# Token lists of a mixture-of-experts layer in three groups of experts instead of two, on one Trainium2 core

## What is computed

```python
k = int(CAPACITY_FACTOR * N / E)                          # 4096 / 8 = 512 tokens for each expert
route_prob = jax.nn.softmax(xf @ Ws + bs, axis=-1).T
route_vals, routes = jax.lax.top_k(route_prob, k)         # the token lists
xin = xf[routes]
h = jax.nn.gelu(jnp.einsum('ekd,edf->ekf', xin, W1) + b1[:, None, :])
out = jnp.einsum('ekf,efd->ekd', h, W2) + b2[:, None, :]
out = out * route_vals[..., None]
final = jnp.zeros((N, D)).at[routes.reshape(-1)].add(out.reshape(-1, D))
```

## Time and profile before

| | |
|---|---|
| device time, median of 3 | 803.45 us (801.62 to 807.27) |
| span of the profiled execution | 760.2 us |
| PE / DVE / ACT / POOL busy | 92% / 66% / 46% / 33% |
| search and places | end near 520.6 us of the span |
| one-hots and lists | 520.65 to 536.4 us |
| first half-width products of expert 0 | from 536.49 us |

### The profile page before, as it was taken

How to read it: one execution, slowest core, us unless ns; L and a number is a source line. 1 busy time by engine, 2 the same in 40 slices (tenths; PEclk the granted TensorE clock), 3 DMA queues, 4 the chain that set the end, 5 groups by cost and what they waited for, 6 DMA issues and landing times.

```text
span 760.2 us, 25608 instructions
## 1 busy us (share of the span) xinstructions
PE 695.7 (92%) x11058; PEld 618.6 (81%) x11058; DVE 501.5 (66%) x1159; ACT 348.2 (46%) x765; POOL 247.4 (33%) x358
## 2 busy tenths in 40 slices
PE   7998998999989999999999999508999999999993
PEld 6886787989978999899899888407689998999992
DVE  6716774555446678777767677678378878877820
ACT  2663544445544546655656564530353345325410
POOL 5510044555644413223140431001734253203333
PEclk9998999999999999999999998755899999999997
DMA  7960024343443635454544453720735255312213
GB/s 201 391 276 2 31 99 153 109 135 124 157 149 112 196 96 158 135 165 140 168 109 142 138 164 108 262 49 3 233 130 154 54 156 139 120 21 28 29 21 36
DMA packets 75467, 96.81 MB, mean 127 GB/s; under 512 B 11337, under 2 KB 67057, under 8 KB 74202
## 3 DMA queue, kind: packets, MB, share of 16 engines
q1 hardware_dynamic: 62250, 69.52, 28.0%
q0 software_dynamic: 12288, 25.12, 13.2%
q10 hardware_dynamic: 816, 0.53, 0.2%
HBM read 53.78 MB, written 41.55 MB: 125 GB/s over the span
## 4 chain that ended last, share of the span: by engine, by line
PE 78%; DVE 10%; issue 4%; DMA 3%; POOL 2%; ACT 1%; POOLq 0%; DVEq 0%
PE bank L1828 41%; PE attn L1828 27%; PE bank L1786 3%; PE bank L1880 2%; DVE arena L1488 2%; PE bank L1887 1%; DMA arena<-x_p,idxs 1%; PE attn L2189 1%; DMA big<-o_m,gidx 1%; DVE st L1043 1%; PE attn L1771 1%; PE attn L1990 1%; POOL arena L524 1%; POOL big L467 1%; DVE big L1056 1%
## 5 line engine op out<-in xcount | busy, mean ns | idle before, releaser
L1828 PE MATMUL attn<-arena 32*32 32x64 f32 (+4 forms) x6048 | 140.3, 225 | 9.2 <-issue 7.3
L1828 PE MATMUL bank<-xT,arena 128*128 128x128 f32 (+2 forms) x964 | 145.8, 306 | 0.0
L1828 PEld LDWEIGHTS attn<-arena 32*32 32x32 f32 (+3 forms) x6048 | 114.2, 120 | 33.2 <-issue 15.4
L1828 PEld LDWEIGHTS bank<-xT,arena 128*128 128x128 f32 x964 | 124.3, 192 | 11.2 <-issue 5.8
L467 POOL DMA_INDIRECT big<-o_m,gidx x64 | 71.0, 1109 | 159.7 <-PE bank L1828 116.9
L460 POOL DMA_INDIRECT x_c<-big,sidx x64 | 68.6, 1071 | 119.3 <-PE bank L1828 88.9
L1828 PE MATMUL bank<-arena,xT 128*128 128x128 f32 (+2 forms) x640 | 107.1, 320 | 0.1
L1828 PEld LDWEIGHTS bank<-arena,xT 128*128 128x128 f32 x640 | 90.0, 199 | 8.6 <-issue 2.9
L543 POOL DMA_INDIRECT out_dram<-arena,idxs x32 | 50.2, 1569 | 109.6 <-ACT arena L1010 99.3
L1165 DVE COPY_PREDICATED arena<-causal,attn 128x1024 f32<-128x1024 int32 x24 | 31.6, 1316 | 71.2 <-PE attn L1828 71.2
L524 POOL DMA_INDIRECT arena<-x_p,idxs x32 | 34.3, 1070 | 98.8 <-DVE idxs L1567 70.8
(11 more groups left out here) (305 smaller groups left out, 1249.2 us busy)
## 6 DMA issues: line engine op xcount, KB each, us to landing
x_c<-zeros SPq DMA_DIRECT2D x8, 1024.0 KB, 9.2
xT<-x_c SPq DMA_DIRECT2D x16, 512.0 KB, 4.1
o_m<-arena SPq DMA_DIRECT2D x16, 512.0 KB, 4.0
xT<-in_L_ffn_W_dram SPq DMA_DIRECT2D x8, 1024.0 KB, 7.9
gs<-in_L_ffn_W_dram SPq DMA_DIRECT2D x8, 1024.0 KB, 7.6
xT<-in_L_attn_x_dram SPq DMA_DIRECT2D x8, 512.0 KB, 5.2
out_dram<-xT SPq DMA_DIRECT2D x8, 512.0 KB, 5.2
arena<-in_L_attn_x_dram SPq DMA_DIRECT2D x7, 512.0 KB, 6.2
```

The lines of the kernel that those rows point to most:

```text
L1828: return nc.tensor.matmul(out_, l, r, start=a, stop=z, skip_group_check=True)
```

## The change

There are three groups: expert 0 alone, experts 1 to 3, and experts 4 to 7. The table of a group is copied (`by_digits`) inside the next group's first `one_hots`, between the high digit's one-hot and the multiplication by the token number. The tables go to banks 4, 5 and 3, and expert 0's first products to banks 4 to 7, so that they no longer share banks 2 and 3 with the lists. PE does the second half of group 2's table and its `spread` inside `first_hidden`, and the wait for all lists moves from before the first half product to before `rows_t(1)`.

```diff
-LISTS = ((0, 4), (4, 8))
+LISTS = ((0, 1), (1, 4), (4, 8))
...
-                    nc.scalar.activation(ht[:, 0, f, :], bank[2 + f % 4][:, :], ACT.Gelu_apprx_tanh,
+                    nc.scalar.activation(ht[:, 0, f, :], bank[4 + f % 4][:, :], ACT.Gelu_apprx_tanh,
...
-            def one_hots(q, h):
+            def one_hots(q, h, after_digits=lambda: None):
...
                                         over_e(number[:, :, at], hi - lo), ALU.is_equal)
+                after_digits()
                 dve.wait_ge(s_low, 2 * q + h + 1)
...
-            for q in range(NL):
-                for h in range(2):
-                    one_hots(q, h)
-                    if q and h == 0:
-                        by_digits(q - 1)
-                        token_list(q - 1)
+            one_hots(0, 0)
+            one_hots(0, 1)
+            for q in range(1, NL):
+                one_hots(q, 0, lambda: by_digits(q - 1))
+                token_list(q - 1)
+                one_hots(q, 1)
             by_digits(NL - 1)
             token_list(NL - 1)
...
             by_lists(1, 0)
             warm(5, bank[7])
             by_lists(1, 1)
+            warm(5, bank[7])
+            spread(1)
+            by_lists(2, 0)
             warm(8, bank[7])
...
-                    ins = mm(bank[2 + f][:, t], w1s[0][:, k, P * f:P * f + P], xet[:, 0, k, t], k == 0, k == 1)
+                    ins = mm(bank[4 + f][:, t], w1s[0][:, k, P * f:P * f + P], xet[:, 0, k, t], k == 0, k == 1)
...
                 first_rows_t(0)
-                spread(1)
-                warm(6, bank[5])
-                pe.wait_ge(s_list, NL)
+                by_lists(2, 1)
                 pe.wait_ge(e_xt, 1)
                 hidden_half(0, 0)
                 hidden_half(1, 0)
+                spread(2)
                 first_rows_t(1)
                 hidden_half(2, 0)
+                pe.wait_ge(e_xt, 2)
+                for f in range(3):
+                    hidden_half(f, 1)
                 hidden_half(3, 0)
-                pe.wait_ge(e_xt, 2)
-                for f in range(4):
-                    hidden_half(f, 1)
+                hidden_half(3, 1)
+                pe.wait_ge(s_list, NL)
                 rows_t(1)
...
                 if n:
                     pe.wait_ge(h_c, 3 * n)
-                else:
-                    pe.wait_ge(e_gl, 5)
...
-                if n == 0:
-                    pe.wait_ge(e_gl, 6)
...
+LIST_BANK = (4, 5, 3)
```

More of the change, by code:

```diff
@@ L1561, in by_digits @@
                 dve.wait_ge(s_idx, q + 1)
-                nc.vector.tensor_copy(cidx[0:n * HI, q, 0:n * LO], bank[3 + q][0:n * HI, 0:n * LO]).then_inc(s_idxc, 1)
+                nc.vector.tensor_copy(cidx[0:n * HI, q, 0:n * LO], bank[LIST_BANK[q]][0:n * HI, 0:n * LO]).then_inc(s_idxc, 1)
             def token_list(q):
@@ L2157, in by_lists @@
                 for t in range(NT // 2 * h, NT // 2 * h + NT // 2):
-                    ins = mm(bank[3 + q][0:n * HI, 0:n * LO], oha[:, lo:hi, :, t].rearrange("p e c -> p (e c)"),
+                    ins = mm(bank[LIST_BANK[q]][0:n * HI, 0:n * LO], oha[:, lo:hi, :, t].rearrange("p e c -> p (e c)"),
                              ohb[:, lo:hi, :, t].rearrange("p e c -> p (e c)"), t == 0, t == NT - 1)
@@ L2226, in first_hidden @@
                     for k in range(2):
-                        ins = mm(bank[2 + f % 4][:, :], w1s[0][:, k, P * f:P * f + P], xet[:, 0, k, :], k == 0, k == 1)
+                        ins = mm(bank[4 + f % 4][:, :], w1s[0][:, k, P * f:P * f + P], xet[:, 0, k, :], k == 0, k == 1)
                     ins.then_inc(e_h, 1)
```

## The result

| | before | changed |
|---|---|---|
| median of 9 executions, us | 803.45 (800.79 to 807.27) | 798.11 (792.21 to 799.49) |
| ratio, with its 95% interval (the two medians alone give 0.9934) | | 0.9923 (0.9902 to 0.9943) |
| profiled execution: own time / span, us | not recorded / 760.2 | 799.49 / 797.7 |

The account below looks back on a forecast made before the run. PE was taken as the bound, with a 1.09 us wait for expert 1's gather before its steady stretch. Its queue, re-added, brought expert 1's transposes from 546.40 to 545.1: 803.45 − 1.3 = 802.1 us, range 799.4 to 804.8.

Parts of the forecast that it names:

- the 43.25 us between lie outside the span and are not touched: Whole run: the difference between the 760.2 us span and the 803.45 us median was held to stay unchanged.
- The narrow product: Expert 0's table on PE: 0.034 us per 32-column product, scaled from 128 columns; 1.1 us for 32.
- First list and first gather: DVE's first list at 524.65, 3.9 us earlier at its end; POOL's first gather at 525.65.
- The 96-column product: Table of experts 1 to 3 on PE: 16 products at 0.102 us each, from 526.65 to 528.3.
- The copy of table 1 waits for nothing: DVE, inside group 2's one-hots: PE's products end at 528.3, one-hots at 528.4, so the copy has no wait.
- The sum: PE's queue from 529.3: half products from 535.7, expert 1's transposes at 545.1 instead of 546.40; −1.3 us, chance 0.50.
- The last table's first half: PE's products for the first half of group 2's table: start at 529.3, take 2.17 us, end at 531.5.
- rival 3: PE's clock rises later than 539, making half products slower; up to 807.3 us, chance 0.13.
- rival 1: POOL's gathers slowed by DVE's one-hots, landing at 546.7; no change, 803.7 us; chance 0.20 together with another rival.
- Hidden edits: Side effects costed at nothing: warm products taken out, a later last list, removed waits, weight transfers 0.3 us earlier.
- The last list: DVE's list for group 2: about 539.4, 3.0 us later, hidden by DVE idle time up to 6.4 us.
- The removed waits: The two waits of hidden(0) for the GELU of f = 4 and 5: cost nothing before, rows done by 552.

Follow-up runs that it names:

- e1: Kernel before, run again unchanged in a set at about 764 us; ratio against itself 1.0013 (0.9987 to 1.0038).
- e9: Kernel before with expert 0's first products in banks 4 to 7 and the lists' wait moved behind the half products; ratio 0.9952 (0.9923 to 0.9980).
- e11: Changed kernel with spread(2) and the lists' wait put back ahead of the first half product; ratio to the kernel before 0.9981 (0.9954 to 1.0008).
- e5: Kernel before, unchanged, one profiled execution in a set at about 800 us; 800.15 us.
- e2: Changed kernel, run again unchanged in a set at about 764 us; ratio to the kernel before 1.0002 (0.998 to 1.0023).
- e7: Changed kernel with group 1's products taking 128 columns instead of 96; 794.41 us, ratio to the kernel before 0.9927 (0.9903 to 0.9952).
- e18: Changed kernel, unchanged, run beside e17 in a set at about 764 us; ratio to the kernel before 1.0014 (0.9991 to 1.0037).
- e3: Kernel before with only expert 0's first products in banks 4 to 7 and two waits of hidden(0) removed; ratio 1.0013 (0.9988 to 1.0038).
- e10: The kernel of e3, lists' wait still ahead of the half products, in a set at about 800 us; ratio to the kernel before 0.9982 (0.9960 to 1.0003).
- e12: Kernel before, unchanged, one execution for a second trace at about 800 us; half products at +21.2, expert 1's transposes at +31.5.
- e14: Kernel before with POOL waiting for the last list after six of the eight gathers; ratio 0.9966 (0.9938 to 0.9995).
- e17: The kernel of e9 run beside the changed one in a set at about 764 us; ratio to the kernel before 0.9996 (0.9971 to 1.0021).

## Why the prediction was wrong

**The step that failed first** was "the 43.25 us between lie outside the span and are not touched". They lay inside the timed executions, and among them were the 5 us that the change takes away. The prediction had no price for the wait for the lists. In its profile the half products began 0.06 us after the last list's end (536.43, and 536.49), with no idle time of PE, and it never asked what the wait would cost if that list were late. The list's row in the profile before, which follows its spread as promptly as in e1:

```profile
536.26 0.17 DVE L1567 TENSOR_SCALAR idxs<-attn 128x16 int32<-128x16 f32 x1 [2.76 <-PE attn L1828]
```

At the 800 level the same list starts at +20.9 instead of +15.6. Moving that wait is what wins: e9 alone gains 3.8 us (0.9952 of 800.03), e11 takes the changed kernel's gain back to 0.9981.

The rest of the 43 us is mostly not in this stage. The spans of e5 and e1 differ by 36.5 us (798.4 and 761.9), and 31.1 of them lie in front of the first one-hot (553.66 and 522.59). PE's waits that no engine ends, at the 800 level (the changed kernel) and then at the 764 level (e2), here with their number and the longest, all lie in front of the first one-hot:

```profile
PE attn L1829 <- issue: 19.7, 41, 1.3
```

```profile
PE attn L1829 <- issue: 7.2, 5, 3.0
```

These waits differ by 12.5 us; where the rest of the 31 us lies isn't known.

**The narrow product** was put at 0.034 us and took 0.062 (1.99 for 32). Its copy came at +3.2, predicted +3.15: PE left the warm products 0.8 us earlier and so paid for it. First list and first gather came 0.2 us before the forecast.

**The 96-column product** was the term of the sum that was mis-sized: 0.102 us predicted, 0.177 measured (2.83 for 16), where 128 columns take 0.136. "The copy of table 1 waits for nothing" was therefore wrong by 2.40 us. The Trainium skill (TensorE: Matmul & The Clock Gate, Weight-path perf modes — Fast Weight Load (FWL) and DoubleRow) says that the fast load is used only when there are 128 weights and the input isn't float32. The trace agrees: float16 products of 32, 96 and 128 columns took 0.062, 0.177 and 0.134 us (with 16, 48 and 64 moving columns). By that rule 32 and 96 columns scale with each other (0.062·3 = 0.186) and not with 128, and it was the prediction's scaling from 128 that broke it. e7, with 128 columns and 0.109 us each, brings the half products at +14.2, and the forecast was +15.05.

**The sum.** The last table's first half began at +10.7, 2.1 us behind the forecast of 529.3 (+8.65), because of the 96-column products. From there to the half products PE took 5.6 us (568.75 to 574.36) and not 6.4: the sum added up durations of rows that overlap, where their distances from start to start are shorter, and this error gave 0.8 us back. So the half products stood at +16.3 against +15.05 predicted, 0.5 us later than before and not 0.8 earlier. The transposes of expert 1 had no idle time in front of them, as forecast, but stood at +26.0 against +24.45. At one level the stage was worth nothing (+25.8 before, +25.8 and +27.6 in e2 and e18), not −1.3 us.

**The clock** (rival 3). The windows of the changed kernel, of 1 us each, PEclk before the last two numbers:

```profile
577.00:578.00 1.00, 1.00 (x5) 0.35 (x4) 0.00 (x0) 0.00 (x0) 0.00 (x0) 0.50 0.02 4
578.00:579.00 1.00, 1.00 (x39) 0.96 (x39) 0.46 (x2) 0.06 (x1) 0.00 (x0) 0.94 0.00 0
```

It rose from 1.2 to 2.4 GHz near +20, before near +18.3. So rival 3 happened in part: all eight records of the row at 574.36 ran at the lower level, as forecast, and the spread as well. The 24 behind cost 0.227 us each, so it was no 5 us.

**Gathers under one-hots** (rival 1). The first gathers took 1.35, 1.90, 1.00, 1.59 and 1.72 us, those when DVE was idle 1.00. The mechanism was right and harmless: the last of expert 1 ended at +17.5, and PE came for its rows 8.5 us later, without a wait. The 1.50 us of expert 1's last gather before, which also ran beside a sum of DVE, spoke for the rival too and was left out there. What the Trainium skill (SBUF — State Buffer, Who interferes with whom) says of VectorE instructions with two SBUF inputs agrees with these rows: a gather behind one was up to 0.9 us longer.

**Hidden edits.** The last list came at +20.5, later than the forecast of 539.4 (+18.75), and DVE still had 1.81 us of idle time in front of `token_sums(1)`. The removed waits cost nothing either way (e3: 1.0013).

**Still open.** The changed kernel had 0.9923, 0.9913 and 0.9910 in three sets, e9 0.9952 in a fourth. Their intervals overlap; whether the groups add 2 to 3 us at the 800 level isn't settled. In the stage itself they add nothing (transposes at +26.1 in e9 and +25.9 to +26.1 in the changed kernel), nor behind it (213.7 us to the end in e9, 213.7 to 213.8 in the changed kernel). Nor is it settled why a signal of PE waits there for the end of POOL's gathers: some other signals of PE did arrive during gathers, such as the one to the copy at 574.58 of the changed kernel, 0.07 us into its eighth gather. And what makes a set one of 764 or 800 us isn't known.

## What to carry to other kernels

Compare the profiled span with the time of the same execution before anything else. If tens of microseconds are missing, the profile is of other circumstances, and every wait with a slack of a few tenths needs a price of its own for the case that it ends late. A wait should stand right in front of what needs its data: here a change of banks let it move behind 32 records of PE, which costs nothing where the list is in time and saves about 4 us where it isn't (e9). Cutting a table into narrower ones doesn't scale a product's cost by its columns: the one with 96 cost more than the one with 128. And a queue of overlapping rows is added up from start to start, not by durations.

## What the hardware showed that I had not expected

A signal from PE reached DVE and ACT only 1.06 to 1.3 us after the last of a run of gathers on POOL, in five profiled executions at the 800 level (e5, e9, e10, e12, e14), and in none of the same layout at the 764 level (before, e1, e3, e17). The router's addition after the experts' scores shows a similar wait. In e5, where its engine sat idle until (us, times):

```profile
  remote: 13.9, 4
```

And in e1:

```profile
  PE attn L1828: 5.2, 4
```

It is 3.5 us a time instead of 1.3; in its first case in e5, DVE started 0.9 us after a gather had ended and 1.7 us after PE's product. Whether the gathers are the cause there too was not tried.
